# Message sums of a graph layer: all 24 edge tiles of a turn gathered by GpSimd, none fetched row by row by SyncE and ScalarE

## The reference

```python
h = jax.nn.relu(x @ w1 + b1)
msg = ew[:, None] * h[src]
agg = jax.ops.segment_sum(msg, dst, num_segments=x.shape[0])
h = agg @ w2 + b2
return jax.nn.relu(_bn(h, g, b))
```

## Time and profile before

| | |
|---|---|
| median of 3 executions | 5181.58 us |
| lowest, highest | 5176.66, 5183.23 us |
| profiled execution, span from first to last instruction | 7408.6 us |
| mean granted TensorE clock in it | 0.687 of full speed |
| busy share of the span: TensorE, VectorE, ScalarE, GpSimd | 48%, 42%, 11%, 50% |
| DMA issues in the two sum phases: gathers on line 858 | 2,996 |
| single rows on line 808, from SyncE and from ScalarE | 8,320 each |
| offset columns on line 794, from SyncE and from ScalarE | 132 each |

### The profile page before, as it was taken

The page is one execution under the profiler, slowest core; times in us unless marked ns, Lnnn a source line. Parts: engine busy times, 40 slices in busy tenths (PEclk is TensorE's granted clock), DMA queues, the critical chain, the costliest instruction groups (busy, mean ns, idle before and its releaser), DMA issues. The chain is left out here.

```text
span 7408.6 us, 125636 instructions
## 1 busy us (share of the span) xinstructions
PE 3524.7 (48%) x20036; PEld 3259.3 (44%) x20037; DVE 3079.5 (42%) x9295; ACT 832.6 (11%) x1874; POOL 3709.9 (50%) x3766
## 2 busy tenths in 40 slices
PE   6344444433334444354444444343344343549999
PEld 5333333333334333354333333333333333438998
DVE  6333333333333333453333333333333335655665
ACT  4000000000000000130000000000000002444444
POOL 3544444444444444354444444444444442557777
PEclk9666666666666666676666666666666666559999
DMA  6222222222222222132222222222222222634444
GB/s 173 73 69 70 68 68 71 71 71 68 69 72 69 69 69 68 56 99 72 70 68 68 68 71 72 70 68 68 70 69 70 71 68 63 151 85 74 78 77 76
DMA packets 371980, 559.26 MB, mean 75 GB/s; under 512 B 137057, under 2 KB 266753, under 8 KB 371778
## 3 DMA queue, kind: packets, MB, share of 16 engines
q0 software_dynamic: 190848, 449.23, 23.1%
q1 hardware_dynamic: 141090, 87.80, 4.8%
q10 hardware_dynamic: 39968, 21.44, 1.1%
HBM read 477.60 MB, written 80.47 MB: 75 GB/s over the span
## 5 line engine op out<-in xcount | busy, mean ns | idle before, releaser
L858 POOL DMA_INDIRECT c_messages<-h,c_indices x2996 | 2833.2, 946 | 3071.9 <-DVE c_indices L938 2215.5
L905 PE MATMUL c_partial<-c_onehot,c_messages 128*128 128x128 f32 x12504 | 2273.5, 351 | 3509.4 <-issue 2159.8
L905 PEld LDWEIGHTS c_partial<-c_onehot,c_messages 128*128 128x128 f32 x12504 | 2096.5, 258 | 3682.8 <-issue 2321.5
L956 DVE TENSOR_TENSOR sums<-sums,c_partial 128x256 f32 x3126 | 1317.4, 421 | 3774.0 <-remote 2005.3
L923 DVE TENSOR_SCALAR c_onehot<-iota,edge_dst,edge_w 128x128 f32<-128x128 f32 x3136 | 1110.9, 355 | 0.1
L844 ACT ACTIVATE sums<-c_z,columns 128x192 f32 x256 | 93.6, 416 | 5819.8 <-issue 5819.8
L1884 POOL DMA_INDIRECT out<-ffn_result,ffn_table x210 | 335.7, 1599 | 97.1 <-issue 56.2
L1925 PE MATMUL ffn_ps<-ffn_xT,ffn_w_tile 128*128 128x256 f32 x1680 | 382.0, 381 | 0.0
L1925 PEld LDWEIGHTS ffn_ps<-ffn_xT,ffn_w_tile 128*128 128x128 f32 x1680 | 312.6, 191 | 38.5
L1568 POOL DMA_INDIRECT table<-rt_entry,rt_slot x196 | 187.8, 958 | 182.4 <-DVE rt_slot L1716 126.5
L1867 POOL DMA_INDIRECT ffn_rows<-tokens,ffn_table x218 | 231.8, 1064 | 67.9 <-issue 61.6
(11 more groups left out here) (189 smaller groups left out, 2492.2 us busy)
## 6 DMA issues: line engine op xcount, KB each, us to landing
c_messages<-h ACTq DMA_DIRECT2D x8320, 1.0 KB
c_messages<-h SPq DMA_DIRECT2D x8320, 1.0 KB
c_messages<-h,c_indices POOLq DMA_INDIRECT x2996
x<-in_x SPq DMA_DIRECT2D x28, 896.0 KB, 6.4
h<-pi_h ACTq DMA_DIRECT2D x14, 896.0 KB
out<-rt_x SPq DMA_DIRECT2D x14, 896.0 KB
tokens<-rt_tokens SPq DMA_DIRECT2D x14, 896.0 KB
h<-ph_h SPq DMA_DIRECT2D x24, 512.0 KB
```

Source lines behind the costliest of these rows:

```text
L858: pool.indirect_dma_start(messages[:, k, :], None, source, bass.IndirectOffsetOnAxis(ap=indices[:, k:k + 1], axis=0)).then_inc(s_message[k ...
L905: last = pe.matmul(partial[:, k % TURN_BANKS, g * P:(g + 1) * P], messages[:, slot, g * P:(g + 1) * P], onehot[:, k % TURN_ONEHOTS, :], st ...
L956: dve.tensor_tensor(where, where, partial[:, k % TURN_BANKS, 0:C].rearrange("p (g n) -> p g n", g=CG), ALU.add).then_inc(s_added, 1)
```

## The change

`FETCHED` goes, and the second half of a turn becomes tiles 12 to 23. GpSimd gathers 24 tiles a turn where it gathered 23, and VectorE copies 12 indices where it copied 11, after tile 23 and no longer after tile 22. SyncE issues no DMA in the sum phases any more; it only waits for their end. ScalarE keeps the bias of the chunks and nothing else. `messages` has 24 slots where it had 25; `row_index`, `row_offset` (with its one instruction in the planning phase) and the semaphores of the rows and columns go. TensorE waits before tile 23 as before any other tile, and its loop body holds one turn where it held two. The first turn and the 3 tiles left over, the products, the one-hots, the additions and the chunks are as they were.

```diff
 TURN = 24
-FETCHED = TURN - 1
-HALVES = ((0, 12), (12, FETCHED))
+HALVES = ((0, 12), (12, TURN))
...
-                if (a, c1) == (0, K):
-                    dve.wait_ge(s_out, g + 1)
-                    dve.tensor_scalar(t["row_offset"][:], t["edge_src"][:, FETCHED:FETCHED + TURNS * TURN + 1:TURN],
-                                      float(ROW_BYTES), None, ALU.mult)
...
-        messages = sb("messages", [P, TURN + 1, C], F32)
-        row_index = sb("row_index", [1, 2, SHARE], I32)
+        messages = sb("messages", [P, TURN, C], F32)
...
-        s_message = [sem(f"s_message{k}") for k in range(FETCHED)]
-        s_row = [[sem(f"s_row_{e}{u}") for u in range(2)] for e in ("sp", "act")]
-        s_column = [sem("s_column_sp"), sem("s_column_act")]
+        s_message = [sem(f"s_message{k}") for k in range(TURN)]
...
-        def fetch_column(eng, b, turn):
...
-        def fetch_batch(eng, regs, b, batch, place):
...
-        def fetch_rows(eng, regs, b, turn, place):
...
         @block.sync
         def _(sp):
-            fetch_column(sp, 0, 0)
-            fetch_rows(sp, regs, 0, 0, 0)
-            with sp.Fori(0, TURNS // 2) as i:
-                fetch_rows(sp, regs, 0, i * 2 + 1, 1)
-                fetch_rows(sp, regs, 0, i * 2 + 2, 0)
-
-            sp.wait_ge(s_column[0], 16 * (TURNS + 1))
             sp.wait_ge(s_added, TURN_BANKS + EDGE_TILES)

         @block.scalar
         def _(act):
-            fetch_column(act, 1, 0)
-
-            def add_bias(chunk):
+            with act.Fori(0, TURNS - 1) as chunk:
                 gate(act, s_z_stats, CG + (chunk + 1) * CG, passed)
                 for co in range(CG):
                     act.activation(sums[:, co, bass.ds(chunk * Z_COLS, Z_COLS)], z[:, co, :], ACT.Identity,
                                    bias=t["columns"][:, 0, co:co + 1]).then_inc(s_z_biased, 1)
-            fetch_rows(act, regs, 1, 0, 0)
-            with act.Fori(0, TURNS // 2) as i:
-                fetch_rows(act, regs, 1, i * 2 + 1, 1)
-                add_bias(i * 2)
-                fetch_rows(act, regs, 1, i * 2 + 2, 0)
-                add_bias(i * 2 + 1)
...
-                    slot = FETCHED + place if k == FETCHED else k
...
-                    if k == FETCHED:
-                        for b in range(2):
-                            pe.wait_ge(s_row[b][place], round_ * (16 * SHARE) + 16 * SHARE)
-                    else:
-                        pe.wait_ge(s_message[k], i * 16 + 16)
+                    pe.wait_ge(s_message[k], i * 16 + 16)
...
             turn_of(0, TURN, False)
-            with pe.Fori(0, TURNS // 2) as i:
-                turn_of(i * 2 + 1, TURN, True, 1, i)
-                turn_of(i * 2 + 2, TURN, True, 0, i + 1)
+            with pe.Fori(1, TURNS) as i:
+                turn_of(i, TURN, True)
```

More of the change, by code:

```diff
@@ L50 @@
 STEPS_LEFT = EDGE_TILES - TURNS * TURN
[L51 to L56, removed]
+assert TURN % TURN_BANKS == 0 and TURN % TURN_ONEHOTS == 0
+assert 0 < STEPS_LEFT <= TURN_BANKS and STEPS_LEFT <= HALVES[0][1]
 ALL_ROUNDS = EDGE_ROWS // RING
@@ L787, in sum_by_turns @@
         sums = t["sums"]
-        source_bytes = source.rearrange("(a n) c -> a (n c)", a=1).bitcast(U8)
         block = ctx.enter_context(nc.Block())
-        def fetch_column(eng, b, turn):
[L793 to L800, removed]
-        def fetch_batch(eng, regs, b, batch, place):
[L804 to L809, removed]
-        def fetch_rows(eng, regs, b, turn, place):
[L813 to L821, removed]
         @block.sync
         def _(sp):
-            regs = [sp.alloc_register(f"{name}_row{n}") for n in range(ROW_BATCH)]
-            fetch_column(sp, 0, 0)
-            fetch_rows(sp, regs, 0, 0, 0)
-            with sp.Fori(0, TURNS // 2) as i:
-                fetch_rows(sp, regs, 0, i * 2 + 1, 1)
-                fetch_rows(sp, regs, 0, i * 2 + 2, 0)
-            sp.wait_ge(s_column[0], 16 * (TURNS + 1))
             sp.wait_ge(s_added, TURN_BANKS + EDGE_TILES)
@@ L836, in _ @@
         def _(act):
-            regs = [act.alloc_register(f"{name}_row{n}") for n in range(ROW_BATCH)]
-            fetch_column(act, 1, 0)
-            def add_bias(chunk):
+            with act.Fori(0, TURNS - 1) as chunk:
                 gate(act, s_z_stats, CG + (chunk + 1) * CG, passed)
@@ L845, in add_bias @@
                                    bias=t["columns"][:, 0, co:co + 1]).then_inc(s_z_biased, 1)
-            fetch_rows(act, regs, 1, 0, 0)
-            with act.Fori(0, TURNS // 2) as i:
-                fetch_rows(act, regs, 1, i * 2 + 1, 1)
-                add_bias(i * 2)
-                fetch_rows(act, regs, 1, i * 2 + 2, 0)
-                add_bias(i * 2 + 1)
-            act.wait_ge(s_column[1], 16 * (TURNS + 1))
         @block.gpsimd
@@ L887, in product_of, with turn_of @@
                 last.then_inc(s_z, 1)
-            def turn_of(i, steps, with_chunk, place=0, round_=0):
+            def turn_of(i, steps, with_chunk):
                 for k in range(steps):
                     n = i * TURN + k
-                    slot = FETCHED + place if k == FETCHED else k
                     if k == Z_PRODUCT and with_chunk:
@@ L898, in turn_of @@
                     pe.wait_ge(s_added, n + 1)
-                    if k == FETCHED:
-                        for b in range(2):
-                            pe.wait_ge(s_row[b][place], round_ * (16 * SHARE) + 16 * SHARE)
-                    else:
-                        pe.wait_ge(s_message[k], i * 16 + 16)
+                    pe.wait_ge(s_message[k], i * 16 + 16)
                     for g in range(CG):
                         last = pe.matmul(partial[:, k % TURN_BANKS, g * P:(g + 1) * P],
-                                         messages[:, slot, g * P:(g + 1) * P], onehot[:, k % TURN_ONEHOTS, :],
+                                         messages[:, k, g * P:(g + 1) * P], onehot[:, k % TURN_ONEHOTS, :],
                                          start=True, stop=True)
@@ L2098, in kernel_program @@
                 t[name] = held(name, [P, STEP_ROOM], dt)
-            t["row_offset"] = held("row_offset", [P, TURNS + 1], I32)
             t["step_nodes"] = held("step_nodes", [1, EDGE_ROWS], I32)
```

## The result

The changed kernel takes **5339.9 us** (median of 4 executions, 5337.9 to 5340.9), the kernel before 5181.5. The ratio is 1.0307, 95% interval 1.0295 to 1.0320: **158 us slower**, where 160 were predicted. The chips do not all behave alike here: on the chip of the last four runs the kernel before took 7344 us and the changed one 6615. The first profile of the kernel before, with its 7409 us, looks like that chip's. Experiments 5 and 9 to 12 are about it.

What follows compares the result with a forecast made beforehand. GpSimd's gathers were taken to bound the turn at 28.2 us. One gather more a turn adds 160 us and the other parts nothing: 5181.6 + 160 = 5342 us, 3.1% slower, range 5305 to 5378, lower end then set to 5290.

Steps and rivals of the forecast that it cites:

- GpSimd bounds the turn: Sum phases: 23 gathers at 1.25 us take 28.75 us, within 2% of the 28.2 us turn; no other engine comes as near.
- The added gather, 162.5 us by the rows, 160 taken: GpSimd, one gather more a turn: 65 x 2 x 1.25 = 162.5 us; scaled by 28.2 / 23, 159.6.
- rival (c): Row fetches slow the gathers before, 1.20 us without them in place of 1.228: 5260 us; chance 0.03.
- If the other stages take 1494.0 in both: Stages outside the sum phases, profiled and timed alike; leaves the sum phases 3687.6 us, then 28.2 us a turn.
- The row fetches' turn, 26.1 us: ScalarE's chain of register loads, row batches and bias, under GpSimd's 28.2 with 2 us to spare.
- The wait for tile 23 and the later indices: Second index copy comes after tile 23 in place of 22; GpSimd does not wait: cost nothing, cover 10 us.
- rival (d): GpSimd waits for its indices each turn; if 3 us stay, 5732 us; chance 0.02.
- The Trainium skill's rule on VectorE and GpSimd's port: Added gathers could cost 130 x 3.1 = 403 us; prediction held the trace does not agree for this kernel's operations.
- Rival (b): Transfers cover the issue time and bytes stay the same, so nothing changes: 5182 us; chance 0.03.
- The profile after: Changed kernel: 3,126 gathers, 1.25 us apart, no TensorE waits for rows; profiled span falls to 5400 to 6950 us.

Runs made afterwards that it cites:

- 9 to 12: On one chip: changed kernel 6615.1 us; 24 gathers and rows 8039.8; 20 gathers, rows, bias between batches 6867.8; turns of 22, bias between 7831.6; kernel before 7343.9.
- experiments 1, 2 and 4: Changed kernel with one gather a turn fewer, no rows: 5181.0 us; kernel before with 24 gathers and all row fetches: 5348.6 us; the third is under experiment 4.
- experiment 4: Changed kernel with 20 gathers a turn and no row fetches, tiles 20 to 23 multiplied from tile 19's slot: 4698.7 us, ratio 0.9062 to the kernel before.
- experiment 5: The kernel before, unchanged, profiled once more: 5187.6 us, span 5185.9.
- experiment 3: Kernel before with 20 gathers a turn, tile 23 still fetched by rows: 4969.4 us, ratio 0.9584 to the kernel before.
- experiment 7: Changed kernel with one more unread float32 VectorE copy for each tile: 5422.6 us, ratio 1.0463 to the kernel before.

## Why the prediction was right

- **GpSimd bounds the turn.** Right, by experiments 1, 2 and 4, and by the gapless timeline after.
- **The added gather, 162.5 us by the rows, 160 taken.** The traces give 2 x (1954.2 - 1875.1) = 158.2 us in the sum phases. 65 gathers a layer at 1.25 are 81.3, so the gathers before were 2 us a layer longer in all. If that is rival (c), it has 4 us where it had 78; but the two profiles were not taken together, and gathers without rows differ by as much (experiment 4), so it is not shown.
- **"If the other stages take 1494.0 in both", 28.2 us a turn.** This step failed, though it moved the sum by 3 us only. The other stages take 1426.5 us after the change and 1433 in experiment 5. The some 65 us between belong to the first profile's execution: on the slow chip the changed kernel too has 1509.5 there. The turn before is 28.8 us, as 23 x 1.25 said. I had scaled a good number by a bad one, and that the scaled 160 lies nearer to the measured 158 than 162.5 does is luck.
- **The row fetches' turn, 26.1 us.** Mis-sized: 27.1 by experiment 3. The margin was about 1.7 us and held.
- **The wait for tile 23 and the later indices, nothing.** Right: rival (d) left no wait of its size.
- **The Trainium skill's rule on VectorE and GpSimd's port** ("SBUF — State Buffer", "SBUF: two separate sides"). That this kernel's own operations leave the gathers alone was right: 946 ns in the median. A copy beside each gather holds up about one in eight (experiment 7), which the rows before could not show.
- **The Trainium skill's rule that the time to initiate a DMA is usually small beside the DMA** ("DMA: Bandwidth & Descriptors", "Issuing engines are not separate DMA queues"). Rival (b), with its sum of 5182, fell: the time went with the issues, at 158 / 130 = 1.22 us for each added gather and 1.24 in experiment 4. The DMA engines are 36% busy in the sum phases.
- **The profile after.** Spacing, count and missing waits came as said. The span was forecast at 5400 to 6950 us, on the idea that the profiler held the engines up beside gathers. The span was 5338.2. The idea was wrong. Nor was it the row fetches alone that stretched the first profile: on the chip that behaves like it the changed kernel, without a row fetch, still has a turn of 39 us and a span of 6612.9. That lies inside the range, but there the *time* fell too. Most likely the first profile was honest about its execution, which ran as long as it says; on which chip it ran is not on record.

## What to carry to other kernels

Where one engine issues equal instructions at an even distance, as the gathers at 1.25 us here, count them: each one moved to idle queues should be worth its full distance until the other queue's turn is reached (27.1 against 28.75 us here), and moving it back costs the same. Here this was measured for one gather in 24, taken back; pushing more to the other queues by shorter turns lost 316 us. A gather's price is the instruction, not its rows (64 rows save 0.044 us of 1.25). When a profile's span and the timed median lie 40% apart, take neither the shares nor the other stages from it: profile again, on another chip too, since a version that is 3% faster on one chip can be 11% slower on the next.

No version that does all the work beat the kernel before on the chips at 5182 us. On the chip at 7344 us the changed kernel did, by 10%.

## What the hardware showed that I had not expected

- A chip on which the kernel before takes 7344 us and the same program 5182 to 5185 on others, with gathers of equal length (946 ns) and TensorE, SyncE and ScalarE slow beside them; the slowness ends 2 to 3 us after the last gather of a stretch.
- An indirect gather of 64 rows takes 0.90 us where one of 128 takes 0.946.
- A float32 copy of 296 ns on VectorE lengthens a gather when it starts within 100 ns of the gather's start (1,082 ns on average), and not when it starts more than 150 ns away (946).
- 128 row DMAs a turn beside the gathers lengthen a gather by 4 ns at most on the usual chips (and it is not shown that they do); on the other chip they add 11 us a turn.
